# One chain of scales for two normalizations on POOL, and two products of the state scan in another place

## The reference

```
# third stage: selective scan (512 channels in, 256 in the scan, 16 states each)
x_ssm, z = split(x @ w_in.T + b_in)
dt = softplus(x_ssm @ w_dt.T + b_dt);  Bm, Cm = x_ssm @ w_B.T + b_B, x_ssm @ w_C.T + b_C
h[n] = exp(dt * A[n]) * h[n] + (dt * x_ssm) * Bm[n]        # for every token, n = 0..15
y = sum over n of h[n] * Cm[n]  + D * x_ssm
pre = (y * silu(z)) @ w_out.T + b_out + residual
x = layernorm(pre) * gamma + beta                           # "norm 3"
# between them, and the fourth stage
x = layernorm(x)                                            # "norm 4"
h = layernorm(x) * ln_gamma + ln_beta                       # "norm 5"
x = x + 0.5 * (silu(h @ w1 + b1) @ w2 + b2)
x = layernorm(x)                                            # "norm 6", the output
```

## Time and profile before

| | us |
|---|---|
| median of 3 runs | 1099.14 |
| lowest, highest | 1098.18, 1101.73 |
| the profiled execution | 1099.67 |
| its span in the trace | 1097.8 |

### The profile page before, as it was taken

The page is one execution under the profiler, slowest core; times in us unless marked ns, Lnnn a source line. Parts: engine busy times, 40 slices in busy tenths (PEclk is TensorE's granted clock), DMA queues, the critical chain, the costliest instruction groups (busy, mean ns, idle before and its releaser), DMA issues. The chain is left out here.

```text
span 1097.8 us, 17984 instructions
## 1 busy us (share of the span) xinstructions
PE 981.0 (89%) x5598; PEld 744.3 (68%) x5598; DVE 935.5 (85%) x1232; ACT 848.0 (77%) x1664; POOL 720.4 (66%) x623
## 2 busy tenths in 40 slices
PE   6999999999969999998748699899999989896887
PEld 4777777777755555555536587777777777775676
DVE  7999999999964897856899999999999999899751
ACT  7778878877736667767767798898998989796743
POOL 3456567766761111314789988999999998988630
PEclk9999999999998999999878699999999999899999
DMA  6443434433405001114979575566776757666201
GB/s 192 121 139 115 136 107 140 121 111 100 138 30 193 1 20 59 38 39 114 243 155 195 139 154 138 138 163 129 186 149 166 148 144 162 147 145 143 71 8 38
DMA packets 93921, 133.86 MB, mean 122 GB/s; under 512 B 8706, under 2 KB 48642, under 8 KB 93828
## 3 DMA queue, kind: packets, MB, share of 16 engines
q1 hardware_dynamic: 93828, 132.73, 48.0%
HBM read 116.45 MB, written 14.16 MB: 119 GB/s over the span
## 5 line engine op out<-in xcount | busy, mean ns | idle before, releaser
L2339 DVE TENSOR_TENSOR_SCAN ob<-bank_a,h,ob 128x512 f32<-128x512 f32 x128 | 160.2, 1268 | 14.8 <-ACT bank_a L2006 10.1
L2339 DVE TENSOR_TENSOR_SCAN oa<-bank_a,h,oa 128x512 f32<-128x512 f32 x128 | 160.3, 1269 | 13.1 <-ACT h L2015 6.7
L1491 POOL TENSOR_TENSOR oa<-ob,x1T 128x1024 f32<-128x1024 f32 x8 | 18.8, 2353 | 129.4 <-DVE ob L1391 129.4
L1815 PE MATMUL bank_m<-w,f_h 128*128 128x256 f32 x448 | 102.9, 379 | 0.0
L2006 ACT ACTIVATE bank_a<-s,A 128x512 f32<-128x512 f32 x128 | 86.9, 685 | 15.5 <-DVE ob L2339 8.7
L2006 ACT ACTIVATE bank_a<-dtc,A 128x512 f32<-128x512 f32 x128 | 86.8, 684 | 12.7 <-DVE oa L2339 6.3
L1760 PE MATMUL bank_y<-ident,ob 128*128 128x128 f32 x512 | 71.9, 287 | 25.1 <-DVE ob L2345 13.2
L1815 PEld LDWEIGHTS bank_m<-w,f_h 128*128 128x128 f32 x448 | 83.6, 190 | 13.9 <-issue 3.6
L1760 PEld LDWEIGHTS bank_y<-ident,ob 128*128 128x128 f32 x512 | 62.8, 148 | 36.4 <-DVE ob L2345 15.8
L1760 PE MATMUL bank_y<-ident,oa 128*128 128x128 f32 x512 | 74.0, 292 | 12.4 <-DVE oa L2345 12.4
L883 POOL TENSOR_TENSOR xd<-xs,L 128x512 f32<-128x512 f32 x32 | 34.0, 1061 | 76.9 <-DVE xs L662 76.9
(11 more groups left out here) (407 smaller groups left out, 2933.0 us busy)
## 6 DMA issues: line engine op xcount, KB each, us to landing
Bb<-CB_rows SPq DMA_DIRECT2D x128, 256.0 KB, 5.6
Cb<-CB_rows SPq DMA_DIRECT2D x128, 256.0 KB, 5.0
...
```

The source lines that it names most:

```text
L1815: i = e.matmul(to, f_h[:, k, c * CH:(c + 1) * CH], w2[:, k, :], start=False, stop=(c % 2 == 1 and k == KF - 1))
L2339: e.tensor_tensor_scan(s[:, k, :], p_a[k][:, :], s[:, k, :], h0[:, n, k:k + 1], ALU.mult, ALU.add).then_inc(v_s, 1)
```

## The change

Three things are changed.

1. **One chain of scales.** `norm6(old)` and `norm3(post)` on POOL, two chains of four small operations, become `norm36`: one chain on tiles of 8 columns (`ve36`, `rs36`, `nb36`), in passes 3 to 7. The order inside a chain is another: the mean times -1 is taken right behind the variance, so that the chain has three stages that wait for each other and not four. In passes 1 and 2, where there is only norm 3, and for block 5 in pass 8, the chain runs alone on 4 columns in the new order. ACT's and DVE's waits for norm 6 follow POOL's count of norm 3 there.
2. **Product of state 3 on POOL.** State 3 joins `on_pool`. DVE no longer makes it and ACT no longer spreads its C. On POOL it stands between `into(cur, 6)` and `into(cur, 7)`. `into(cur, 7)` writes the buffer that it reads. `load_C` of state 7 now waits for POOL's product.
3. **Product of state 1 ahead of the residual sum** on DVE.

```diff
@@ the scales' tiles
+            st36, st4 = t("st36", [P, 2, 2, 2, 3]), t("st4", [P, 2, 2, 3])
+            ve36, rs36, nb36 = (t(n, [P, 2 * NC]) for n in ("ve36", "rs36", "nb36"))
...
+            alone = {NB - 3: 0, NB - 2: 1}
...
-            p_g, on_pool = d_sem("p_g"), (0, 12, 14)
+            p_g, on_pool = d_sem("p_g"), (0, 3, 12, 14)
@@ ACT
                 def norm6(b, p):
-                    e.wait_ge(p_l6, 4 * b + 4)
+                    if b in alone:
+                        e.wait_ge(p_l6, 4 * alone[b] + 4)
+                    else:
+                        e.wait_ge(p_l3, 4 * (b + 2) + 4)
...
                         decay(cur, 4, 1)
-                        spread_C(cur, 3)
                         carry(cur, 3)
@@ DVE
+                    if live(cur):
+                        product(cur, 1)
                     if 0 <= post < NB - 1:
                         residual(post, 0)
-                    if live(cur):
-                        product(cur, 1)
...
                         scan(cur, 4, 0)
                         scan(cur, 4, 1)
-                        product(cur, 3)
                         scan(cur, 5, 0)
@@ POOL
+                def scales(parts, done, base):
+                    e.sem_inc(step, 1)
+                    e.tensor_scalar(ve36[:, parts], mv36[:, parts, 1], 1.0 / DM, EPS, ALU.mult, ALU.add).then_inc(done, 1)
+                    e.tensor_scalar(nb36[:, parts], mv36[:, parts, 0], -1.0, None, ALU.mult).then_inc(done, 1)
+                    e.wait_ge(done, base + 1)
+                    e.sem_inc(step, 1)
+                    e.tensor_tensor(rs36[:, parts], ve36[:, parts], mhalf[:, parts], ALU.pow).then_inc(done, 1)
+                    e.wait_ge(done, base + 3)
+                    e.sem_inc(step, 1)
+                    e.tensor_tensor(nb36[:, parts], nb36[:, parts], rs36[:, parts], ALU.mult).then_inc(done, 1)
...
+                def norm36(b3, b6):
+                    e.wait_ge(v_l6, 2 * b6 + 2)
+                    e.wait_ge(v_l3, 2 * b3 + 2)
+                    scales(slice(0, 2 * NC), p_l3, 4 * b3)
...
-                    if 0 <= old < NB - 2:
+                    if old in alone and live(post):
                         norm6(old)
-                    if 0 <= post < NB - 1:
+                    elif old >= 0 and 0 <= post < NB - 1:
+                        norm36(post, old)
+                    elif 0 <= post < NB - 1:
                         norm3(post)
                     if live(cur):
                         into(cur, 6)
+                        product(cur, 3)
                         into(cur, 7)
```

More of the change, by code:

```diff
@@ L54, in build @@
         ident, ones = (sb(n, [P, P]) for n in ("ident", "ones"))
-        mhalf, sign = sb("mhalf", [P, NC]), sb("sign", [P, 1])
+        mhalf, sign = sb("mhalf", [P, 2 * NC]), sb("sign", [P, 1])
         px = ctx.enter_context(ExitStack())
@@ L916, in norm @@
                     e.sem_inc(step, 1)
-                    e.tensor_tensor(rs[:, :], ve[:, :], mhalf[:, :], ALU.pow).then_inc(p_ln, 1)
+                    e.tensor_tensor(rs[:, :], ve[:, :], mhalf[:, 0:NC], ALU.pow).then_inc(p_ln, 1)
                     e.wait_ge(p_ln, 4 * b + 2)
@@ L2378, in stats6 @@
                     e.wait_ge(v_x3b, 2 * b + p + 1)
-                    after(e, p_l6, 4 * b)
+                    if b - 1 in alone:
+                        e.wait_ge(p_l6, 4 * alone[b - 1] + 4)
+                    elif b > 0:
+                        e.wait_ge(p_l3, 4 * (b + 1) + 4)
                     e.bn_stats(both_of(st6, p), turnwise(x3b, p)).then_inc(v_l6, 1)
@@ L2446, in end_second @@
                     e.tensor_scalar(ve6[:, half[p]], mv6[:, half[p], 1], 1.0 / DM, EPS, ALU.mult, ALU.add).then_inc(v_e, 1)
-                    e.wait_ge(p_l6, 4 * Z + p + 1)
+                    e.wait_ge(p_l6, 4 * len(alone) + p + 1)
                     e.scalar_tensor_tensor(nb6[:, half[p]], mv6[:, half[p], 0], -1.0, rs6[:, half[p]], ALU.mult, ALU.mult).then_inc(v_b, 1)
@@ L2588, in norm3 @@
-                    e.tensor_tensor(nb3[:, :], mv3[:, :, 0], rs3[:, :], ALU.mult).then_inc(p_l3, 1)
-                    e.wait_ge(p_l3, 4 * b + 3)
-                    e.sem_inc(step, 1)
-                    e.tensor_scalar(nb3[:, :], nb3[:, :], -1.0, None, ALU.mult).then_inc(p_l3, 1)
+                    scales(slice(0, NC), p_l3, 4 * b)
                 def norm6(b):
                     e.wait_ge(v_l6, 2 * b + 2)
-                    e.sem_inc(step, 1)
-                    e.tensor_scalar(ve6[:, :], mv6[:, :, 1], 1.0 / DM, EPS, ALU.mult, ALU.add).then_inc(p_l6, 1)
@@ L2597, in norm6 @@
-                    e.wait_ge(p_l6, 4 * b + 1)
-                    e.sem_inc(step, 1)
-                    e.tensor_tensor(rs6[:, :], ve6[:, :], mhalf[:, :], ALU.pow).then_inc(p_l6, 1)
-                    e.wait_ge(p_l6, 4 * b + 2)
-                    e.sem_inc(step, 1)
-                    e.tensor_tensor(nb6[:, :], mv6[:, :, 0], rs6[:, :], ALU.mult).then_inc(p_l6, 1)
-                    e.wait_ge(p_l6, 4 * b + 3)
-                    e.sem_inc(step, 1)
-                    e.tensor_scalar(nb6[:, :], nb6[:, :], -1.0, None, ALU.mult).then_inc(p_l6, 1)
+                    scales(slice(NC, 2 * NC), p_l6, 4 * alone[b])
```

21 lines of the change are left out of this document (7 added, 14 removed).

## The result

| | before | after |
|---|---|---|
| median of 7 runs each, us | 1099.15 | 1105.93 |
| lowest, highest | 1097.94, 1103.05 | 1103.11, 1107.37 |
| ratio, 95% interval | | 1.0044 [1.0027, 1.0061] |
| the profiled execution | 1099.67 | 1105.93 |
| its span | 1097.8 | 1104.1 |

By the ratio the change makes the kernel slower by 4.8 us (0.0044 x 1099.15), with 3 to 6.7 as the interval. The prediction had 4.0 us more than before, 1103.1; the measured median is 2.8 us above that, just inside the 1106 at which the forecast's own range ended.

A forecast was written before the change was run, and what follows sets the result against it. It took POOL from `shifted` to the scales of norms 4 and 5, then ACT's norm 5, then DVE, as the bound. Delays of `scaled` summed to +3.93 us on 1099.67, 1103.6, adjusted to 1103.1; the forecast's own range was 1100 to 1106.

The forecast's parts named there:

- What bounds it: POOL from `shifted` to the scales of norms 4 and 5, then ACT's norm 5, then DVE, sets the end.
- Part 1: Joined chain on POOL: 2.50 us for 4.51, gaining 2.01 in passes 3 to 7; 0.39 in passes 1 and 2.
- Part 2 on POOL: Product 3 ahead of `into` 7 costs POOL 2.62 us, its 0.25 of handover included.
- DVE's part at nothing: DVE loses 1.19 us of work per pass but gains 0.3 at most before product 5; costed at nothing.
- a sign of being wrong: PE's `add_up` of state 3 waiting for POOL was named among the signs that the forecast is wrong.
- SP at nothing: Load of B for state 9 goes out 5 us later, lands in 5.6, some 3 us left; costed at nothing.
- The rival of late loads: Loads of C 7 and B 9 land late and stop `into` 9, from landings of some 8.5 us: 1107; chance 0.1.
- The sum by pass: Delay of `scaled` on POOL in each pass, added work less earlier waits: together +3.93 us, pass 0 at 0.
- One sign I had named: DVE idle ahead of the scans of state 11 in passes 1 to 3 and 6, as a sign of being right.
- Pass 0: POOL's product fills `into` 7's 1.67 us load wait; between -1.2 and +1.0 us, taken as 0.
- The rival of a draw: POOL's added work meets waits behind norm 5, or the 8-column power costs hardly more: +1, 1100 us; chance 0.25.
- DVE as the bound: Rival: DVE's shorter list pulls all else forward, up to -9.5 us, 1089.6, or 1095 at half; chance 0.13.

The follow-up runs named there:

- `p2_product3`: The kernel before with product 3 moved to POOL and the two chains of scales left as they were: 1113.15 us, ratio 1.0121.
- `q3_after_45`: The kernel after with the scales of norms 4 and 5 also joined in one chain on POOL: 1092.82 us, 0.993 against the kernel before.
- `p1_chain`: The kernel before with only the joined chain of norms 6 and 3; products 3 and 1 as before: 1097.77 us, ratio 0.9981.
- `q4_p13_45`: The kernel before with both chains joined (norms 6 and 3, norms 4 and 5) and product 1 first, product 3 left on DVE: 1093.40 us, 0.9931.
- `q2_dve_light`: The kernel before with DVE's product of state 3 made on 2 of 512 columns, waits and orders kept: 1098.10 us, ratio 0.9976.
- `p0_wide`: The kernel before with only the constant tile of -1/2 widened to 8 columns, which moves the tiles behind it: ratio 0.9992.
- `p3_product1`: The kernel before with only the product of state 1 put ahead of the residual sum on DVE: 1099.57 us, ratio 0.999.
- `r4_p12`: The kernel after with product 1 back behind the first half of the residual sum on DVE: 1103.73 us, 1.0031 against the kernel before.

## Why the prediction came out right, and where it did not

**What bounds it: right for work that is added, and only in part for work taken away.** The chain from `shifted` to the scales of norms 4 and 5 decides. What is put on POOL there is paid in full: 14.1 us in the trace of `p2_product3`, of 14.6 by the prediction's sum. Once product 3 is on POOL, what is taken away comes back in full too: 1.69 us in each pass (`q3_after_45`), and the joined chain's 9.9. With product 3 on DVE, ACT is soon the later one: 2.1 us of 9.6 (`p1_chain`) and 5.5 of 11.8 (`q4_p13_45`) come through, no larger a share than the 2.6 of 8.6 for work taken off DVE (`q2_dve_light`) in the one case, and a larger one in the other. Whether work taken off DVE pays in the kernel after was not tried.

**Part 1: right.** The power on 8 columns takes 1.67 us against my 1.69, and the page's row over all five is the same:

```profile
L2592 POOL TENSOR_TENSOR rs<-ve,mhalf 128x8 f32<-128x8 f32 x5 | 8.3, 1665 | 0.0
```

The chain takes 2.59 against 2.50, since the operation with -1 is not free after all: it stands between the power and the chain's first operation, and the power starts 0.49 behind that (732.29 - 731.80) and not 0.38. Two slips of the working did no harm. The gain's lower bound should have been 4.51 - 0.81 - 2.08 = 1.6, not 1.4. And the scales of norm 6 are not ready earlier than before but 0.3 later behind the chain's start (the first of the two chains took 727.62 - 725.35 = 2.27, the joined one 2.59); ACT's norm 6 waits for POOL in none of passes 3 to 7 in either trace.

**Part 2 on POOL: right**, 2.62 us as in the earlier trace rows. **DVE's part at nothing: right for passes 2 to 5.** `add_up` of state 3 keeps its place there, as I had written: in pass 3 PE starts it at 739.88, straight behind other work of its own and 0.80 us after POOL's product has ended (739.08). Product 5 waits 0.51 for it, and DVE gains 0.16 us, with 0.3 allowed. In `q2_dve_light`, where POOL has no product 3, the wait is 0.51 as well. In passes 1, 6 and 7 there stands what I had named as a sign of being wrong: PE waits for POOL's product 3, for 4.55, 0.56 and 5.01 us, and product 5 waits behind it for 3.09, 1.29 and 1.37. Pass 1:

```profile
608.19 1.97 PE L1763 MATMUL bank_y<-ident,oa 128*128 128x128 f32 x8 [4.55 <-POOL oa L2579]
```

```profile
610.30 1.22 DVE L2350 TENSOR_TENSOR oa<-ob,bank_c 128x1024 f32<-128x1024 f32 x1 [3.09 <-PE bank_y L1763]
```

In these passes too norm 5 then waits for POOL (1.39, 2.02 and 1.94), so POOL stayed the later one. **SP at nothing: right for the passes 3 to 7**, where no `into` 9 waits for a load, and wrong in that loads take 7.5 us and not 5.6. The rival of late loads had 8.5 as its point of decision, and that was not reached in the median; the waits for loads in pass 0 and at the start of pass 1 are of its kind.

**The sum by pass** held, against the trace that it was made from. From `shifted` to `scaled`:

| pass | 1 | 2 | 3 | 4 | 5 | 6 | 7 | sum |
|---|---|---|---|---|---|---|---|---|
| forecast | +1.54 | +0.86 | +0.61 | -0.34 | +0.04 | +0.61 | +0.61 | +3.93 |
| measured | +1.53 | +0.93 | +0.70 | -0.40 | +0.08 | +0.68 | +0.38 | +3.90 |

The kernel after takes 11.6 to 12.4 us in each pass, so the forecast had POOL's added work right. How long the kernel before waits there is another matter, and I took it from one execution: the sum of 80.90 is 82.35 in `p0_wide` and 83.45 in `p3_product1`, where pass 2 alone takes 12.90 and 12.51 against 10.72. Against the three together the term is +2.9 and not +3.9, so it was too high by about 1 us.

In passes 1, 2, 4 and 5 `scaled` waits no more. In pass 4 it should still have waited 0.12 (1.07 less POOL's 0.61 is 0.46, and ACT comes 0.34 earlier); the chain's 0.09 more and a little else took it. One sign I had named is missing: the scan of state 11 does not wait in pass 2, though norm 5 waits 1.25 for POOL there, and in pass 3 it waits 0.36 only. That part of the chain had slack.

**Pass 0: the term that was mis-sized.** I took 0 between -1.2 and +1.0; it is +3.29 in this pair of traces and +2.1 in the mean of all. The step that failed is "since both lean on `into` 7": I had looked at what waits for `into` 7 and not at what waits for the product itself (`add_up`, then product 5), nor at the loads behind it, in pass 0 and at the start of pass 1, for which POOL waited then.

**Between the blocks: no gain.** From `scaled` to the next `shifted` the kernel after is 2.52 us shorter in the pair of traces, 2.13 of it between passes 6 and 7. There the trace of the kernel before waits longest for a load, at `into` 3 of pass 7:

```profile
976.03 2.37 POOL L2565 TENSOR_TENSOR ob<-s,Bb 128x1024 f32<-128x1024 f32 x1 [2.62 <-DMA Bb<-CB_rows]
```

But the same instruction of the same order of work waits 0.81 in `p0_wide`, and 0.79 in `p3_product1`:

```profile
975.51 2.37 POOL L2565 TENSOR_TENSOR ob<-s,Bb 128x1024 f32<-128x1024 f32 x1 [0.81 <-DMA Bb<-CB_rows]
```

In the kernel after it is 1.02:

```profile
982.06 2.37 POOL L2572 TENSOR_TENSOR ob<-s,Bb 128x1024 f32<-128x1024 f32 x1 [1.02 <-DMA Bb<-CB_rows]
```

So the 2.62 is one late load of one execution, and the change gains nothing here, as costed. The rival of a draw, waits behind norm 5 that do not move along, has nothing from it.

**The total, partly by luck.** Two terms were off, in opposite directions: pass 0, at 0 where it costs 2.1 to 2.6 us, and the passes, too high by about 1. What remained, 1.1 to 1.6 us, is within the scatter of the runs. What the experiments bear out is the mechanism for passes 1 to 7; that the sum came out near the result is luck in part.

**DVE as the bound, and the product's price.** The first falls with `q2_dve_light`. Of the second: 2.36 us on POOL against 1.20 on DVE, as the Trainium skill (GPSIMD Engine Reference, Engine selection) has it with a factor of two, is what the engine pays; what the kernel pays was between nothing that can be measured (with both chains short, `q3_after_45` against `q4_p13_45`), 5.5 us (with the first short, `r4_p12` against `p1_chain`) and 13.3 us for eight products (with both long, `p2_product3`).
